# Masked attention of a four-layer network: in layers 0 and 3 the mask of one head pair in four is added by VectorE instead of TensorE

## The reference

```python
scores = jnp.einsum('bhqd,bhkd->bhqk', Q, K) / np.sqrt(D_K)
scores = jnp.where(mask[:, None, :, :] == 0, NEG, scores)
attn = jax.nn.softmax(scores, axis=-1)
ctx = jnp.einsum('bhqk,bhkd->bhqd', attn, V)
return ctx.transpose(0, 2, 1, 3).reshape(b, sq, D_MODEL) @ wo + bo
```

## Time and profile before

| | |
|---|---|
| median of three runs | 4367.12 us (4364.86 to 4370.69) |
| the profiled execution | 4376.57 us, its span 4374.7 us |
| PE, busy share of the span | 81% |
| DVE | 58% |
| ACT | 40% |
| mean granted clock of TensorE | 0.895 |

### The profile page before, as it was taken

The page is one execution under the profiler, slowest core; times in us unless marked ns, Lnnn a source line. Parts: engine busy times, 40 slices in busy tenths (PEclk is TensorE's granted clock), DMA queues, the critical chain, the costliest instruction groups (busy, mean ns, idle before and its releaser), DMA issues. The chain is left out here.

```text
span 4374.7 us, 68566 instructions
## 1 busy us (share of the span) xinstructions
PE 3537.7 (81%) x18821; PEld 1770.6 (40%) x18821; DVE 2556.5 (58%) x7436; ACT 1760.6 (40%) x2506; POOL 1149.3 (26%) x1239
## 2 busy tenths in 40 slices
PE   3999999897399899969957777776538999996697
PEld 1343343343133333336634444444313434335465
DVE  4665665776487777853125555555666666663531
ACT  0454455443044344441125545555433445552111
POOL 2334430001445444401022222221222212201132
PEclk7999999898699999979978888888658999996799
DMA  5543540001454344310048888888332432313133
GB/s 109 84 68 62 77 73 12 19 1 42 72 93 83 74 83 78 73 46 0 0 104 223 231 231 220 232 232 229 125 56 35 56 49 35 49 16 107 46 99 68
DMA packets 211868, 392.82 MB, mean 90 GB/s; under 512 B 24624, under 2 KB 76688, under 8 KB 211360
## 3 DMA queue, kind: packets, MB, share of 16 engines
q1 hardware_dynamic: 205344, 379.99, 39.9%
q0 software_dynamic: 6144, 8.39, 1.1%
HBM read 189.88 MB, written 96.47 MB: 65 GB/s over the span
## 5 line engine op out<-in xcount | busy, mean ns | idle before, releaser
L424 DVE CUSTOM_DVE_ANT_0 A_sums<-A_p_ps,A_bias 128x512 bf16<-128x512 f32 x1536 | 1006.1, 687 | 411.8 <-PE A_p_ps L270 389.4
L497 ACT ACTIVATE A_probs<-A_p_ps 128x1024 f32<-128x1024 f32 x640 | 654.3, 1024 | 613.0 <-PE A_p_ps L289 591.0
L270 PE MATMUL A_p_ps<-A_k_stack,A_q_stack 96*128 96x512 bf16 x1536 | 512.0, 390 | 106.5 <-DVE A_nmax L424 96.4
L284 PE MATMUL A_p_ps<-A_q_stack,A_k_stack 99*128 99x512 bf16 x1536 | 461.9, 382 | 0.1
L299 PE MATMUL A_oT_ps<-A_probs,A_v_aug 128*17 128x512 f32 x3072 | 407.0, 602 | 3.2 <-ACT A_probs L497 2.4
L1082 DVE CUSTOM_DVE_ANT_0 A_scores<-A_qk_ps,A_rel_in 128x384 f32<-128x384 f32 (+3 forms) x512 | 232.7, 486 | 215.6 <-POOL A_rel_in L1151 114.8
L990 PE MATMUL A_t_ps<-ident,A_scores 128*128 128x128 f32 x1280 | 225.3, 315 | 134.5 <-DVE A_probsT L1072 124.7
L270 PEld LDWEIGHTS A_p_ps<-A_k_stack,A_q_stack 96*128 96x128 bf16 x1536 | 135.6, 98 | 486.1 <-DVE A_nmax L424 387.6
L289 PE MATMUL A_p_ps<-A_biasT,ident_bf 128*128 128x512 bf16 x1024 | 307.4, 381 | 0.0
L1072 DVE COPY A_probsT<-A_t_ps 128x1024 f32<-128x1024 f32 (+3 forms) x256 | 210.5, 822 | 120.7 <-PE A_t_ps L990 114.1
L1133 ACT ACTIVATE A_scores<-A_scores,A_nmax 128x384 f32<-128x384 f32 (+3 forms) x512 | 257.9, 555 | 48.5 <-DVE A_nmax L1082 48.3
(11 more groups left out here) (356 smaller groups left out, 5901.6 us busy)
## 6 DMA issues: line engine op xcount, KB each, us to landing
A_k_stack<-A_parts SPq DMA_DIRECT2D x192, 256.0 KB, 8.9
A_q_stack<-A_parts SPq DMA_DIRECT2D x192, 256.0 KB, 9.2
A_rel_dram<-A_rel_out SPq DMA_DIRECT2D x64, 512.0 KB, 4.9
A_rel_in<-A_rel_dram SPq DMA_DIRECT2D x64, 512.0 KB
A_rel_dram<-A_rel_out SPq DMA_DIRECT2D x64, 384.0 KB, 4.4
A_rel_in<-A_rel_dram SPq DMA_DIRECT2D x64, 384.0 KB, 4.4
A_ctxT<-in_ctxT SPq DMA_DIRECT2D x32, 512.0 KB, 12.7
A_mask_in<-in_mask SPq DMA_DIRECT2D x64, 256.0 KB, 3.5
```

The source lines that it names most:

```text
L270: nc.tensor.matmul(p1_ps[i % 2][:, :], q_stack[0:KS, a_par, j * GH + i, t * P:(t + 1) * P], k_stack[0:KS, a_par, j * GH + i, :], start=Tru ...
L284: last = nc.tensor.matmul(p2_ps[half][:, i % 2, :], k_stack[:, par, j * GH + i, kb * P:(kb + 1) * P], q_stack[:, par, j * GH + i, :], star ...
L424: nc.vector.tensor_tensor_reduce(out=sums[:, i % NX, :], in0=p1_ps[i % 2][:, :], in1=bias[:, t, :], scale=-1.0, scalar=3.4028235e38, op0=A ...
L497: nc.scalar.activation(dst, src, ACT.Exp).then_inc(exp_done, 1)
```

## The change

In layers 0 and 3 half 1 of every odd step (positions 3, 7, 11, ... 31, eight in a batch) now does as half 1 of layer 1 does: PE leaves out the two L289 matmuls, DVE adds `biasT` (here bf16) with one instruction behind its two L424, and ACT takes the exponential from SBUF. There are 8 x 8 x 2 = 128 such positions. Layer 1 is left as it is. A wait on `exp_done` for the two banks of half 1 becomes a wait on `biased` where DVE read them, and POOL, which rewrites `biasT` for the next batch, also waits for the last add.

```diff
-        BY_DVE = (1,) if adj is not None else ()
+
+        EVERY = 1 if adj is not None else 2
...
-        def adds(step):
-
-            return step * len(BY_DVE)
+        def by_dve(s, half):
+            return half == 1 and s % EVERY == EVERY - 1
+
+        def adds(b, s):
+
+            return b * (STEPS // EVERY) + (s + 1) // EVERY
...
-                    if half in BY_DVE:
+                    if by_dve(s - 1, half):
                         if later(b * STEPS + s):
-                            pe.wait_ge(biased, adds(b * STEPS + s - 1) + BY_DVE.index(half) + 1)
+                            pe.wait_ge(biased, adds(b, s - 1))
                     elif later(b * STEPS + s):
                         pe.wait_ge(exp_done, b * HALVES + p - 1)
                     for i in pair:
                         last = nc.tensor.matmul(p2_ps[half][:, i % 2, :], k_stack[:, par, j * GH + i, kb * P:(kb + 1) * P],
-                                                q_stack[:, par, j * GH + i, :], start=True, stop=half in BY_DVE)
-                    if half not in BY_DVE:
+                                                q_stack[:, par, j * GH + i, :], start=True, stop=by_dve(s, half))
+                    if not by_dve(s, half):
...
-                if has(b, s) and half in BY_DVE:
+                if has(b, s) and by_dve(s, half):
...
-                    if half in BY_DVE:
-                        act.wait_ge(biased, adds(b * STEPS + s) + BY_DVE.index(half) + 1)
+                    if by_dve(s, half):
+                        act.wait_ge(biased, adds(b, s))
                         src = dst
...
-                if BY_DVE:
-                    pool.wait_ge(biased, adds(done)).then_inc(apart_pool, 1)
+                pool.wait_ge(biased, adds(bn - 1, (NG - 1) * TPB + k % TPB)).then_inc(apart_pool, 1)
```

## The result

The changed kernel takes 4465.25 us (median of four runs, 4461.95 to 4470.19), the kernel before 4365.99 us (four runs, 4363.15 to 4370.69): a ratio of 1.0227, 95% interval 1.0209 to 1.0245. The forecast was 4451 us with a range of 4419 to 4478, so it is slower as forecast, 14 us above the number and inside the range. The profiled execution took 4461.95 us with a span of 4460.1, which is 85.4 us more than the span of before.

What follows compares the result with a forecast made beforehand. PE was taken as bound by DVE handing back first-score banks and by ACT's copies. Some +42 us a layer, +84 for two, made the profiled 4376.57 us 4461, and the median 4451 us, range 4419 to 4478.

Steps and rivals of the forecast that it cites:

- two loops: PE waits for DVE to hand back two first-score banks; PE's side work waits for ACT's copy behind an exponential.
- batch 0: First batch, layers 0 and 3: no `out` at 16, so 1.20 becomes 0.58; +6.6 us.
- Positions 15 and 19: Layer 1's stretches laid over layer 0's: 7.30 against 5.90 less 0.2, +1.20 us; 6.46 against 5.61, +0.85.
- Position 27: Stretch 27 to 29: same side work as 19 to 21, `m` then a projection, so the same +0.85 us.
- Position 3: No ACT copy that PE soon waits for, no `o`; between a 0.43 gain and 1.13 loss, taken as +0.50 us.
- Position 7: Statistics and aggregates stand on DVE behind the add, so nothing takes the hold up: the whole +1.13 us.
- rival B: PE is the bound and the relief from its mask matmuls is gained whole: -55 us, 4312 us; chance 0.05.
- The step from the profiled execution to the median: Profiled execution would become 4461 us; the median, taken 9.5 below it, 4451.
- C: Only the bank turn costs, ACT's copies come in time: +8 us a layer, 4384 us; chance 0.06.
- D: DVE's add is dearer than 1.42 us in layers 0 and 3: above 4478 us; chance 0.03.
- E: DVE stands still behind each add, each hold 2.44 us: +168 us, 4619 us; chance 0.01.
- The signs that the prediction named: PE share below 93, L289 768 instructions, side work waiting on ACT, full batches about 7 us longer, layer 1 unchanged.

Runs made afterwards that it cites:

- e1: Changed kernel, but where DVE adds, ACT copies that position's side work ahead of the exponential that waits for the add; 4404.16 us.
- e10: Changed kernel with the add moved to positions 1, 5, 13, 15, 19, 25 and 27, and ACT's copy ahead of the waiting exponential; 4342.71 us.
- e12: Changed kernel with the hardware loop over batches 1 to 4 of the masked attentions written out on all five engines; 4427.08 us.
- e15: Changed kernel without the add at position 7, where PE adds the mask again; 4439.50 us.
- e9: Kernel before, with the mask pair of every second step left out in layers 0 and 3 and nothing adding it; 4345.89 us.
- e2: Kernel before, keeping PE's mask pairs, with an extra DVE add of the same size on spare SBUF tiles at the 128 positions; 4451.74 us.

## Why the prediction was right, point by point

Its two loops are the mechanism. e1 takes away one by the order of two instructions of ACT, and 64 of 81.5 us go; e10 moves the add out of the other, and the loss turns into a gain. The sum in numbers, the change in us from one position to two on (batches 1 to 5, layers 0 and 3, the turn counted apart):

| position | predicted | measured |
|---|---|---|
| 3 | +0.50 | -0.4 to +0.2, once -1.5 |
| 7 | +1.13 | +0.8 to +1.4, mostly 1.15 |
| 11 | +1.56 | +1.6 to +1.9, in batch 5 +1.1 |
| 15 | +1.20 | +1.19, in batch 5 +0.9 |
| 19 | +0.85 | +0.85 to +0.89 |
| 23 | +0.58 | +0.3 to +0.7 |
| 27 | +0.85 | +0.8 to +1.6 |
| 31 | +0.58 | +0.3 to +0.6 |
| batch 0 | +6.6 | +1.2 and +6.3 |
| batch 6, batch 7 | +0.6, -1.4 | +0.5 and -0.7, -1.0 |
| into 3, layer 0 | not seen | +0.8 in four batches |
| into 10, clock | not seen | +1.2 to +1.6 in seven batches |
| the turn, all layers | not seen | +7.8 |

- Positions 15 and 19 were read off layer 1 and came out to 0.02 us in batches 1 to 4, and 11 to 0.2 in most. Laying a stretch that already has the changed form over one that has not was the step that bore the prediction.
- Position 27 was set equal to 19, and that was mis-sized. Both have the same side work, but DVE lags more at 27. In layer 0, batch 4, of the kernel after, the add starts 1.52 us behind the second scores of its position at 27 (559.50 and 561.02), and 1.36 at 19 (538.22 and 539.58); in batch 1 it is 1.88. By that much more ACT's copy and PE's `q` are late. Equal side work is not an equal place.
- Position 3 came out near zero, mostly as a small gain. The prediction took a value between its bounds with no row for it. In layer 0 two things that it didn't have meet there, and both are DVE's small instructions of position 2 (L369 to L378, now L373 to L382), some 0.18 us each, that grow while POOL works in SBUF. Before, in batches 1, 2, 4, 5 and 6, the last of them took 2.29 us; in the changed kernel the stretch comes at another moment of POOL's work, the last one is short and the first two grow. Layer 0, batch 5, before and after:

```profile
537.29 0.18 DVE L372 TENSOR_TENSOR A_m_rest<-A_nmax,A_m_parts 128x16 f32<-128x16 f32 x1
538.75 2.29 DVE L378 TENSOR_TENSOR A_m_parts<-A_m_rest,A_m_parts 128x16 bf16<-128x16 f32 x1
538.64 2.36 POOL L511 TENSOR_TENSOR x_sb<-x_sb,A_bo_bc 128x1024 f32<-128x1024 f32 x1
```

```profile
580.67 0.71 DVE L376 TENSOR_TENSOR A_m_rest<-A_nmax,A_m_parts 128x16 f32<-128x16 f32 x1
582.20 0.19 DVE L382 TENSOR_TENSOR A_m_parts<-A_m_rest,A_m_parts 128x16 bf16<-128x16 f32 x1
580.20 1.15 POOL L526 TENSOR_TENSOR A_qk<-A_qk,A_parts 128x512 f32<-128x512 f32 x1
```

  The first two stand ahead of first scores, and so 0.8 us come into position 3 (0.5 to 0.8 in e10 and e12). The short last one gives the single -1.5; in batches 1, 2 and 4 the granted clock, 0.50 to 0.51 at position 3 (in 204 to 207, 296 to 299 and 491 to 494 us of the kernel after), takes most of that back.
- Position 7 was right as a hold, and what it brings about was missing: the prediction looked at who is late next, and not at PE's granted clock, which fell to 0.50 in seven of the twelve batches behind waits of 1.74 to 2.13 us and in none without the add (e15).
- The pair of mask matmuls stands in the sum as 0.43 us, and 128 of them in rival B as 55, and no row of the prediction shows either. The trace of before has the 0.43: in layer 0, batch 4, at position 20, the next matmul starts that much behind the start of the pair. No run shows the 55: e9 gave 35.7.

```profile
500.81 0.60 PE L289 MATMUL A_p_ps<-A_biasT,ident_bf 128*128 128x512 bf16 x2
501.24 1.88 PE L225 MATMUL A_front_ps<-A_ctxT,A_wk 128*128 128x512 f32 x4
```

- The turn was in the trace of before, with 3.3, 8.3 and 7.1 us over the other batches, and the prediction took the batches as alike.
- The layers: 42 was forecast for each, and 39.0 and 43.4 came outside the turn.
- The step from the profiled execution to the median failed. The sum made 4461 of the profiled 4376.57, and the profiled execution of the kernel after took 4461.95. The prediction then took off 9.5, by which the profiled execution of before lies over the median; that of the kernel after doesn't lie over its own (4465.25). This is nearly the whole difference of 14 us: 9.5 and 3.3. In the sum itself the terms that were missing, some 9 us of clock and 7.8 of the turn, were made up by those that were too large, by position 3 and the first batch (where 11 cost 0.7 to 0.8 us and 15 gained 0.2), and by 4.0 us less in stages that the change doesn't touch. That the sum is so near is in part luck; the positions 11, 15, 19 and 7 are not.

Rival B is out by e9, C by the bracket at L222 and by e1, D by the mean of 1220, which is the same in layers 0 and 3, with the bf16 operand, as in layer 1, and E by the next L428, which starts 1.13 us behind the add (517.26, 518.39). The signs that the prediction named have come: PE's share below 93, the waits on ACT's copies (in layer 0, batch 4, 1.52 us for `xT` at 12, 1.35 for `out` at 16, 1.02 for `k` at 20 and 1.17 for `q` at 28), layer 1 as long as before (+0.2 us). One can't be read off this trace: it has 660 of the 768 matmuls that now add the mask, since some records are missing. The trace of e1, where PE's list is the same, has all 768.

## What to carry to other kernels

Before work is moved to an engine that has room, look for the place where it has it: the same add cost up to 2.8 us at position 7 and nothing at seven others (with ACT's copy first), and the engine's busy share tells nothing of that; the idle time ahead of its next instruction, with PE as what ended it, does. An engine that serves two chains in order wants the copy that someone waits for ahead of the instruction that itself waits; here that was worth 64 us. And a stage's repeated batches should be laid over each other before a sum is multiplied by their number: the one that differed hid a loss of 19 us that was there to be had in the kernel before.

## What the runs showed of the hardware that was not expected

- A jump back of a hardware loop let PE stand for up to 8.75 us and DVE for 4.17, with "issue" as what ended it and three packets of the instruction queues in the same time. Written out, the same code has no such stand there.
- An addition on DVE with one input in PSUM took 1211 to 1226 ns in 256 cases, 57 of them for over 0.3 us beside a TENSOR_TENSOR of POOL's. With both inputs in SBUF the median was 1222 and the longest 3182 (e2). Even one of 128x16 is hit. The two lines (min/median/max ns) are of the kernel after and of the kernel before:

```profile
L443 DVE TENSOR_TENSOR A_probs<-A_p_ps,A_biasT x256: 1211/1220/1226, 121.8 to 4032.4; 128x1024 f32<-128x1024 f32 x128
```

```profile
L378 DVE TENSOR_TENSOR A_m_parts<-A_m_rest,A_m_parts x96: 185/187/2300, 103.4 to 3931.3; 128x16 bf16<-128x16 f32 x96
```

  One of the long ones starts at 454.98 in the kernel before and lasts 2.29 us, while POOL adds in SBUF from 454.87 for 2.36. All 14 of this line that take over 0.4 us start while an instruction of POOL's in SBUF is running, but no run took POOL's work away to prove the cause.
- PE's granted clock fell to 0.50 behind waits of 1.74 to 2.13 us at position 9, in seven of twelve batches with the same work. Without the add at 7 (e15) it fell there in none.
